# A graph attention layer's source terms: every one from one-hot products, none gathered row by row

## The reference

```python
xl = (x @ W).reshape(n, H, C)
a_src = jnp.einsum('nhc,hc->nh', xl, att_src)
a_dst = jnp.einsum('nhc,hc->nh', xl, att_dst)
logits = jax.nn.leaky_relu(a_src[src] + a_dst[dst], NEG_SLOPE)
seg_max = jax.ops.segment_max(logits, dst, num_segments=n)
ex = jnp.exp(logits - seg_max[dst])
...
out = jax.ops.segment_sum(msgs, dst, num_segments=n)
```

## Time and profile before

| what | us |
|---|---|
| median of three runs | 7612.53 |
| span of the profiled execution (its own time; nothing around it is shown) | 8827.0 |
| TensorE matmuls busy | 5772.8 (65%) |
| VectorE busy | 4203.1 (48%) |
| GpSimd busy | 4135.2 (47%) |
| GpSimd, the 336 gathers of L2266 | 321.1, 956 ns each |
| logits stage of layer 0, from the first broadcast to L2403 | 1078.9 to 1459.9 |
| logits stage of layer 2, from its first one-hots to L2403 | 4528.8 to 5015.8 |

### The profile page before, as it was taken

How to read it: one execution, slowest core, us unless ns; L and a number is a source line. 1 busy time by engine, 2 the same in 40 slices (tenths; PEclk the granted TensorE clock), 3 DMA queues, 4 the chain that set the end, 5 groups by cost and what they waited for, 6 DMA issues and landing times. The chain is left out here.

```text
span 8827.0 us, 71673 instructions
## 1 busy us (share of the span) xinstructions
PE 5772.8 (65%) x20790; PEld 3543.0 (40%) x20790; DVE 4203.1 (48%) x10631; ACT 1003.1 (11%) x2613; POOL 4135.2 (47%) x4069
## 2 busy tenths in 40 slices
PE   5342526764676666775933767747777777777499
PEld 3231414332563433334721444434444222433387
DVE  7233515667434444445221576676553466344511
ACT  1110100111120000002210012211001000100122
POOL 1664051664346654661644056601763466466133
PEclk9998755786788776556955588868788999655699
DMA  1010112332463332332721133311332566233365
GB/s 51 17 32 12 38 28 94 93 91 61 140 163 93 91 77 80 92 90 77 202 48 32 57 81 89 90 38 44 91 87 63 149 181 180 79 92 91 87 196 172
DMA packets 340393, 787.84 MB, mean 89 GB/s; under 512 B 96775, under 2 KB 197132, under 8 KB 325764
## 3 DMA queue, kind: packets, MB, share of 16 engines
q0 software_dynamic: 213504, 491.66, 22.3%
q1 hardware_dynamic: 126508, 291.60, 9.6%
HBM read 708.94 MB, written 77.24 MB: 89 GB/s over the span
## 5 line engine op out<-in xcount | busy, mean ns | idle before, releaser
L2094 PE MATMUL bank<-arena 128*125 128x256 f32 (+3 forms) x5824 | 2663.4, 567 | 1208.7 <-DMA arena<-TAB,arena 269.6
L2077 POOL DMA_INDIRECT arena<-TAB,arena x2080 | 1996.6, 960 | 1726.9 <-DMA TAB<-arena 706.6
L2094 PEld LDWEIGHTS bank<-arena 128*125 128x125 f32 x5824 | 1200.0, 245 | 2620.4 <-issue 898.2
L2138 DVE TENSOR_TENSOR arena<-bank,arena 125x256 f32 (+3 forms) x2912 | 1352.6, 465 | 1550.0 <-PE bank L2094 990.2
L2077 POOL DMA_INDIRECT arena<-TABa,arena x832 | 861.7, 1036 | 996.3 <-DVEq L138 597.6
L2117 DVE TENSOR_SCALAR arena<-arena 128x125 f32<-128x125 f32 x2080 | 614.5, 296 | 268.6 <-PE bank L2094 115.0
L1714 POOL DMA_INDIRECT REC<-arena x400 | 420.8, 1052 | 421.0 <-DVE arena L1932 301.1
L1319 POOL DMA_INDIRECT SUM<-arena x192 | 307.5, 1602 | 479.8 <-DVE arena L1537 408.2
L337 PE MATMUL bank<-arena 128*125 128x256 f32 (+4 forms) x1600 | 455.7, 433 | 107.4 <-DVE arena L715 37.7
L2266 POOL DMA_INDIRECT arena<-TERMa,arena x336 | 321.1, 956 | 422.6 <-DVEq L138 230.0
L1363 PE MATMUL bank<-arena 128*128 128x256 f32 x2048 | 466.2, 383 | 15.1 <-DVE arena L1525 6.0
(11 more groups left out here) (495 smaller groups left out, 5945.6 us busy)
## 6 DMA issues: line engine op xcount, KB each, us to landing
arena<-L_ffn_pack SPq DMA_DIRECT2D x32, 2054.0 KB
arena<-L_ffn_pack SPq DMA_DIRECT2D x64, 1026.0 KB
arena<-TAB,arena POOLq DMA_INDIRECT x2080
arena<-DLR SPq DMA_DIRECT2D x52, 500.0 KB
arena<-SLR SPq DMA_DIRECT2D x31, 500.0 KB
arena<-TABa,arena POOLq DMA_INDIRECT x832
TAB<-arena SPq DMA_DIRECT2D x20, 625.0 KB
arena<-L_ffn_b SPq DMA_DIRECT2D x96, 128.0 KB
```

The source lines that it names most:

```text
L2077: e.indirect_dma_start(out=m.G[k % RING][:, 0:m.width], out_offset=None, in_=m.table[:, :], in_offset=bass.IndirectOffsetOnAxis(ap=eidx[:, ...
L2094: e.matmul(ps[0:P, 0:m.full], m.S[k % SRING], m.G[k % RING], start=True, stop=True).then_inc(*put("pass_p", m.g, "summed", k))
L2138: e.tensor_tensor(o, banks.of(m.g, "added", k)[0:P, 0:m.full], o, ALU.add).then_inc(*put("pass_v", m.g, "added", k))
```

## The change

All 26 pieces of both layers go by products. The table `terms`, its copy `asT`, its write to DRAM and the 336 gathers are gone, and so are `order` and `looks`: pieces come in their natural order, with SLR, DLR and STR broadcast for each. STR is now broadcast to 125 partitions in place of 25, `big` has 125 rows in place of 25, and so the mask's product is over 125 rows; rows 25 to 124 of its one-hots are zero.

```diff
-            self.big = at(45100, H * T, p=T, dt=BF16)
+            self.big = at(45100, H * T, dt=BF16)
...
     def logits_sp(e, a):
-        for n, i in enumerate(a.order):
-            if n > 2:
-                e.wait_ge(*of(a.g, "looked", a.order[n - 3]))
-            if n == 2:
-                e.wait_ge(*of(a.g, "terms"))
+        for i in range(KC // 16):
+            if i > 2:
+                e.wait_ge(*of(a.g, "looked", i - 3))
+            if i == 2:
                 for x in (1, 2):
                     e.wait_ge(*of(a.g, "adx", 6 * a.H - x))
             for j, src in enumerate((SLR, DLR, STR)):
-                if i >= a.looks and j != 1:
-                    continue
-                e.dma_start(a.pieces[n % 3][j], src.rearrange("r j -> (r j)")[i * 2048:(i + 1) * 2048].partition_broadcast(
-                    (P, P, T)[j])).then_inc(*land("logit_p%d" % (n % 3), a.g, "piece", i))
+                e.dma_start(a.pieces[i % 3][j], src.rearrange("r j -> (r j)")[i * 2048:(i + 1) * 2048].partition_broadcast(
+                    P)).then_inc(*land("logit_p%d" % (i % 3), a.g, "piece", i))
...
     def source_sp(e, a):
-        e.wait_ge(*of(a.g, "term"))
-        e.dma_start(rows(a.terms, P), a.asT).then_inc(*land("gat_u", a.g, "terms"))
...
     def source_dve(e, a):
-        e.tensor_copy(a.asT, a.asN.rearrange("p h t -> p t h")).then_inc(*put("gat_v", a.g, "term"))
...
     def logits_dve(e, a):
-                for j, v in enumerate(a.pieces[n % 3]):
-                    if i >= a.looks and j != 1:
-                        continue
-                    ins = e.tensor_scalar(v, v, iotaP[0:(P, P, T)[j], :], None, ALU.is_equal)
+                for v in a.pieces[i % 3]:
+                    ins = e.tensor_scalar(v, v, iotaP[0:P, :], None, ALU.is_equal)
...
     def logits_pe(e, a):
-            for c in range(16 // per if i < a.looks else 0):
+            for c in range(16 // per):
...
-        logits_pool(e, gats[0])
...
-        logits_pool(e, gats[1])
```

More of the change, by code:

```diff
@@ L2156, in program, with __init__ @@
     class Gat:
-        def __init__(self, g, pre, H, C, eps, ng, w0):
-            self.g, self.pre, self.H, self.C, self.eps, self.looks = g, pre, H, C, eps, KC // 16 - ng
-            self.table, self.terms = dd("TAB" + g, [N, H * (C + 1)]), dd("TERM" + g, [N, H])
+        def __init__(self, g, pre, H, C, eps, w0):
+            self.g, self.pre, self.H, self.C, self.eps = g, pre, H, C, eps
+            self.table = dd("TAB" + g, [N, H * (C + 1)])
             o = S0 + 6250
@@ L2178, in __init__ @@
             self.as3 = [at(44800 + 100 * j, H * T, dt=BF16) for j in range(3)]
-            self.big = at(45100, H * T, p=T, dt=BF16)
+            self.big = at(45100, H * T, dt=BF16)
             self.adx = at(B, 6 * H, KC, p=P, dt=BF16)
-            self.pieces = [[at(38600 + 3072 * i + 1024 * j, 2048, p=(P, P, T)[j], dt=BF16) for j in range(3)]
+            self.pieces = [[at(38600 + 3072 * i + 1024 * j, 2048, dt=BF16) for j in range(3)]
                            for i in range(2)]
             i = XN0 + KC * H
[L2184 to L2189, removed]
+            self.pieces.append([at(i, 2048, p=P, dt=BF16), at(i + 1024, 2048, p=P, dt=BF16), at(27550, 2048, dt=BF16)])
             self.as_ = at(XN0, KC, H, p=128)
@@ L2251, in source_dve @@
         e.wait_ge(*last("gat_v"))
-        e.tensor_copy(a.asT, a.asN.rearrange("p h t -> p t h")).then_inc(*put("gat_v", a.g, "term"))
         settle(e, e.tensor_tensor(a.slN, a.asN, a.adN, ALU.add), "gat_v")
         settle(e, e.scalar_tensor_tensor(out=a.slN, in0=a.slN, scalar=0.2, in1=a.slN, op0=ALU.mult, op1=ALU.max), "gat_v")
-    def logits_pool(e, a):
-        e.wait_ge(*of(a.g, "terms"))
[L2263 to L2268, removed]
-    def logits_sp(e, a):
-        for n, i in enumerate(a.order):
-            if n > 2:
-                e.wait_ge(*of(a.g, "looked", a.order[n - 3]))
-            if n == 2:
-                e.wait_ge(*of(a.g, "terms"))
+    def logits_sp(e, a):
+        for i in range(KC // 16):
+            if i > 2:
+                e.wait_ge(*of(a.g, "looked", i - 3))
+            if i == 2:
                 for x in (1, 2):
@@ L2312, in logits_pe @@
         per = 512 // HT - (1 if H == 4 else 0)
-        for n, i in enumerate(a.order):
-            sl, dl, st = a.pieces[n % 3]
+        for i in range(KC // 16):
+            sl, dl, st = a.pieces[i % 3]
             e.wait_ge(*of(a.g, "hots", i))
-            for c in range(16 // per if i < a.looks else 0):
+            for c in range(16 // per):
                 ps, before = banks.take(a.g, "as", i, c)
@@ L2371, in logits_dve, with hots @@
         per = 512 // HT - (1 if H == 4 else 0)
-        def hots(n):
-            if n < KC // 16:
-                i = a.order[n]
+        def hots(i):
+            if i < KC // 16:
                 e.wait_ge(*of(a.g, "piece", i))
-                for j, v in enumerate(a.pieces[n % 3]):
-                    if i >= a.looks and j != 1:
-                        continue
-                    ins = e.tensor_scalar(v, v, iotaP[0:(P, P, T)[j], :], None, ALU.is_equal)
+                for v in a.pieces[i % 3]:
+                    ins = e.tensor_scalar(v, v, iotaP[0:P, :], None, ALU.is_equal)
                 ins.then_inc(*put("logit_v", a.g, "hots", i))
@@ L2384, in logits_dve @@
         e.wait_ge(*of(a.g, "table"))
-        for n, i in enumerate(a.order):
-            hots(n + 1)
-            for c in range(16 // per if i < a.looks else 0):
+        for i in range(KC // 16):
+            hots(i + 1)
+            for c in range(16 // per):
                 e.wait_ge(*of(a.g, "asmm", i, c))
@@ L2399, in logits_dve @@
                                 ALU.add).then_inc(*put("logit_v", a.g, "ds", i, c))
-        for k in range(KC - 8, KC):
-            e.wait_ge(*of(a.g, "term", k))
         e.wait_ge(*last("logit_v"))
```

5 lines of the change are left out of this document (2 added, 3 removed).

## The result

The changed kernel takes 7759.98 us (median of 4, 7755.88 to 7765.39); beside it the kernel before takes 7614.4 (4 runs). The ratio is 1.0193, 95% interval 1.018 to 1.0205: 145.6 us slower (137 to 156 by the interval), where 219 were forecast.

The account below looks back on a forecast made before the run. With no slow TensorE stretches in ordinary runs, broadcasts were to bound changed layer 0 and TensorE layer 2. Terms +111, +112 and -4 gave +219: 7612.5 + 219 = 7831 us, range 7755 to 7900 (8 in 10).

Parts of the forecast that it names:

- Stages before, without stretches: Logits stages of the kernel before, in runs without slow TensorE stretches: 197.3 us in layer 0, 258.0 in layer 2.
- contention: Gathers and broadcasts share DMA engines, lengthening layer 0's stage before by up to 9 us; 4 were taken off.
- Layer 0, +111: Logits stage of layer 0: broadcasts become the bound at 11.73 us a piece, ending at 1399 instead of 1288.
- The TERM write, -6.5 us: Without the write of `terms` in SyncE's queue, layer 2's stage begins 6.5 us earlier (bounds 0 and 7.5).
- Layer 2, +112: Logits stage of layer 2: TensorE bounds it at 14.33 us a piece, 376.3 us from the first one-hots.
- rival 3: TensorE's clock rises to 2.4 GHz in layer 2, broadcasts bound it, 68 us less: 7763; chance 0.06.
- Rival 2: In layer 2 the mask's extra 0.07 us stays, 15.51 us a piece, +31 us: 7862; chance 0.15.
- The stretches: TensorE at one instruction per 1.40 us beside logits gathers, 401 us together; taken as the recording's, absent from ordinary runs.
- rival 1: The slow TensorE stretches are real in ordinary runs, which gain the profile's 178 us: 7435; chance 0.12.
- A span about 180 us shorter with a median some 220 us longer: Sign in the whole kernel's profile and runs that the recording made the slow TensorE stretches.
- In layer 2 one-hots every 14.3 us with TensorE hardly idle: Sign in layer 2's logits stage of the forecast period, with 0.20 us from each product to the next.
- TensorE idle some 2 us a piece: Sign in layer 0's logits stage: one-hots every 11.7 us wait for STR's DMA, so TensorE idles about 2 us.

Follow-up runs that it names:

- a kernel with the same time in condition A: The kernel before with each logits gather waiting for the one 4 before it instead of 8: 7610.94 us against 7614.46, ratio 0.9994.
- condition A: Comparisons, two with the unedited kernel before measured at 7614 us, no edit making the difference; the changed kernel takes 7759.98 us there.
- condition B: Comparisons in which the unedited kernel before takes 8756 to 8803 us; the changed kernel takes 8547.9 us against 8803.46 there, ratio 0.9716.

## Why the prediction came out as it did

**Stages before, without stretches (197.3 and 258.0): right.** 203.2 and 260.5 in a kernel with the same time in condition A. For the missing 8 us the prediction had set 4 aside, as contention. 1.4 of them are the wait for the last gather; that the others are contention is not shown.

**Layer 0, +111: right.** The period is 11.77 us for 11.73, bound by the broadcasts. The forecast counted from the first broadcast, which now starts here:

```profile
797.39 0.25 SPq L2260 DMA_DIRECT2D arena<-SLR  x1
```

From it the stage takes 1117.51 - 797.39 = 320.1 us, and 320.1 was forecast (1399 - 1078.9). Before it took 1012.87 - 798.02 = 214.9, and 209.1 was forecast. So the change is +105.3, and the missing 6 us are those of the stage before. TensorE's part was mis-sized here as well, without an effect on the time: 9.9 us a piece were reckoned, and it is idle for half of the stage.

**The TERM write, -6.5 us: right.** SyncE's queue around the start of the stage of layer 2, in the changed kernel and in the one of condition A that stands for the kernel before:

```profile
3903.42 16.49 SPq L2210 DMA_DIRECT2D TABa<-arena  x4
3920.25 6.07 SPq L2260 DMA_DIRECT2D arena<-SLR  x1
```

```profile
3818.88 6.49 SPq L2219 DMA_DIRECT2D TERMa<-arena  x1
3825.71 10.76 SPq L2281 DMA_DIRECT2D arena<-SLR  x1
```

From the end of the TAB writes to the first one-hots it is 3945.45 - 3919.91 = 25.5 us now and 3850.48 - 3818.88 = 31.6 with the write, 6.1 less.

**Layer 2, +112: wrong, the term that was mis-sized.** The step that failed is "TensorE is the bound" at 14.33 us per piece at 1.2 GHz. The stage was to take 376.3 us and took 309.5; the change is +49.0 - 6.1 = +43. Two things were missed, both effects of the mask's rows. First the size: I had divided 0.61 us by three products and taken 0.203 for each, but the 0.61 already held the late load of the mask's weights. Equal rows follow each other at 0.166, a chunk takes 0.66 and not 0.813, and 16 of them with the target's 1.32 take 11.9 us, about as much as the broadcasts. This alone is 26 x (14.33 - 11.9) = 63 of the 67 us (an estimate from these rows). Second, rival 3: the clock rises, and a chunk takes 0.34. It had a chance of 0.06, because TensorE was at 0.50 in the row before though it was busy for 163 of 169 us. That row could not speak for the changed kernel: busy time there contained the waits at the change of rows. The rival's time, 7763 against 7760 measured, agrees by luck in part: the clock did rise, to 0.79, but the rival kept 14.33 us for a piece at the lower clock, and with 11.9 there the stage would have ended within a few us of the same time without the clock (an estimate from the same rows, 26 x 0.1 us). Rival 2, 15.51 us a piece, falls: four products take 0.66 us, where it kept 0.887.

**The sum** is then +105.3 + 42.9 = 148 us; measured 145.6, with 137 to 156 as its interval. The forecast of +219 was 73 us too high, nearly all of it by layer 2, and the measured time lies only 5 us inside the range of 7755 to 7900.

**The stretches: absent in the runs that count, but for another reason.** "They belong to the recording" failed. In condition A a recorded run with gathers has none; in condition B the ordinary runs take as long as the recorded ones that have them (8756 against 8764 us). That the forecast's sign came out is therefore luck: it rested on times that happened to be of condition A, and the changed kernel was measured in A as well. In condition B the same change measured -256 us, which the prediction gave to rival 1, at 0.12. The two arguments had holes: the 1214 us were the difference of two conditions, within the some 70 us by which runs of B differ, not the price of a recording, and the pace that depended on nothing named was no sign of one. In condition B rival 1 is what happens: its mechanism gave -178, and -256 was measured, since layer 2 gained more than forecast (-174 and not -111, from the first one-hots). The Trainium skill's rule in "NOTIFIC — the notification-queue block", section "7.1 Overflow: three behaviours, one of which stalls the engine", as the prediction used it, would have needed the stretches to be the recording's; the runs do not bear it out here.

**Signs named beforehand.** "A span about 180 us shorter with a median some 220 us longer" cannot be read as meant: span and median were of different conditions. "In layer 2 one-hots every 14.3 us with TensorE hardly idle" was wrong (11.8, and idle for 63 of 235 us). "TensorE idle some 2 us a piece" in layer 0 was wrong too: 134 of 259 us are some 6 us a piece.

**Open.** What makes condition A or B was not found: the kernels, the inputs and in one case the chip's number are the same. Of the 1142 us between them, the stretches explain 390 (371.3 + 482.5 - 203.2 - 260.5); the rest lies in other stages. In the changed kernel, which has no gathers in its logits, the first one-hots of layer 0 come 278 us later in B than in A, those of layer 2 499 us later, and the span is 787 us longer; only a window of 200 us at the start was read for its cause (below). The kernel before, with 8 in flight, has no profile in condition A: that it has no stretches there follows from its median, 7614.46 against 7610.94 with 4 in flight beside it. And why the clock follows the mask's rows is open: over fewer rows TensorE also has gaps at each change of rows, and no run separates the two.

## What to carry to other kernels

Where a product over few rows stands between products over many, look at the starts one by one and not at a mean: filling the rows with zeros may give back both the gaps and the clock, at the price of what fills them (24 us in layer 0 of the kernel before, where the broadcasts to 125 partitions are slow). Give a broadcast 128 partitions, even where 125 are read. And before a difference between a profiled span and a median is put down to the recording, compare the profiled run's own time with its span: where these agree, the difference is between runs.

## What the runs showed of the hardware that was not expected

- The clock followed the mask's rows. With 25 of 125 rows in every fourth product the granted clock was 0.50 in each logits window of seven kernels; with 125 rows and away from stretches it was 0.63 to 1.00, even where TensorE was busy for less than half of the window (124.69 of 259 us, 0.66).
- In condition B, other engines are slower beside indirect DMAs of GpSimd far from the logits too. The windows of the same 200 us, the kernel before in B and then the changed kernel in A, each of which has 616 matmuls behind it at its start:

```profile
200.00:400.00 200.00, 80.68 (x325) 49.98 (x324) 55.17 (x93) 27.31 (x57) 132.83 (x128) 1.00 0.08 25
```

```profile
200.00:400.00 200.00, 159.63 (x648) 100.06 (x648) 113.97 (x188) 49.44 (x113) 160.06 (x132) 1.00 0.13 42
```

TensorE does 325 matmuls and 648, and the changed kernel itself does 324 there in condition B. VectorE in B waits for something that the view only calls "remote", 15.68 us before one instruction and 92.8 us in this window; in A the window has no such wait:

```profile
262.47 0.42 DVE L1912 SCALAR_TENSOR_TENSOR arena<-bank,arena 125x250 bf16<-125x250 f32 x1 [15.68 <-remote]
```

- A kernel's verdict can change its sign with the condition: 1.0193 in A and 0.9716 in B for the same pair. Both intervals are far narrower than the distance between them.
